# Local attention of a fused transformer kernel: values held stationary, probabilities divided before they are transposed, q's inverse norm applied inside the exponential

## The reference, cut to what matters

```python
q, k, v = split(shift_token(x) @ wqkv)            # 3 x 512 columns
q = l2norm(q) * qs;  k = l2norm(k) * ksc          # norm over the 64 of a head
q, k = rotary_xpos(q, k)                          # q*cos*scale + rotate_half(q)*sin*scale, k likewise
sim  = einsum(q * 8.0, look_around(k))            # 64 queries against 128 keys of two windows
sim  = where(mask, -max, sim)
attn = softmax(sim)
o    = einsum(attn, look_around(v))
x    = x + o @ wo
```

## Time and profile before

| | |
|---|---|
| time, three runs | 1675.93, 1677.23 (median), 1678.6 us |
| the profiled execution's own time | 1680.32 us |
| its span | 1678.5 us |
| PE busy | 1360.0 us (81%) |
| DVE busy | 1211.6 us (72%) |
| POOL busy | 887.5 us (53%) |
| ACT busy | 875.7 us (52%) |
| local attention | two stretches: first projections at 765.2 and 1216.7 us, about 370 us each |

### The profile page before, as it was taken

One profiled execution on the slowest core, in us unless ns is written; L12 is line 12 of the kernel. 1 busy time (PEld: TensorE's weight loads), 2 busy tenths in 40 slices (PEclk: granted clock), 3 DMA queues, 4 the chain that ended last, 5 costly groups with the idle time before them and its releaser, 6 DMA issues. The chain is left out here.

```text
span 1678.5 us, 26415 instructions
## 1 busy us (share of the span) xinstructions
PE 1360.0 (81%) x9350; PEld 645.6 (38%) x9412; DVE 1211.6 (72%) x1912; ACT 875.7 (52%) x1677; POOL 887.5 (53%) x980
## 2 busy tenths in 40 slices
PE   2368989989999775775899999968779999998597
PEld 1112222222222123452555555543335555555333
DVE  6268888888888643346888888858578888888484
ACT  1126666667666563224666666633145666665422
POOL 0866766667676101115877777710087777777000
PEclk9659999999999998887999999998989999999898
DMA  3333332333333101001111111101011111000001
GB/s 90 75 57 70 58 70 58 70 65 69 70 58 70 26 1 50 1 2 36 24 24 24 24 24 24 24 1 41 13 29 24 24 24 24 22 21 22 1 0 52
DMA packets 161398, 61.14 MB, mean 36 GB/s; under 512 B 139722, under 2 KB 153076, under 8 KB 161268
## 3 DMA queue, kind: packets, MB, share of 16 engines
q1 hardware_dynamic: 161268, 59.45, 16.8%
HBM read 8.73 MB, written 2.10 MB: 6 GB/s over the span
## 5 line engine op out<-in xcount | busy, mean ns | idle before, releaser
L642 DVE TENSOR_REDUCE row_max<-max_ps 128x2 f32<-128x1024 f32 x256 | 313.0, 1223 | 73.7 <-PE max_ps L514 72.3
L673 ACT ACTIVATE prob<-scores_ps 128x1024 f32<-128x1024 f32 x256 | 262.1, 1024 | 149.3 <-PE scores_ps L494 145.9
L1628 POOL TENSOR_TENSOR la_turned<-la_raw,lw_rot 128x1024 f32<-128x1024 f32 x64 | 154.9, 2420 | 183.4 <-ACT la_raw L1533 156.9
L1285 PE MATMUL la_ring<-lw_wqkv,la_hT 128*128 128x512 f32 x384 | 200.8, 636 | 46.2 <-DVE la_hT L1402 27.4
L494 PE MATMUL scores_ps<-stack 128*128 128x512 f16 x512 | 156.2, 387 | 41.8 <-ACT prob L673 40.9
L1523 ACT ACTIVATE la_prob<-la_s,la_neg_max 128x128 f32<-128x128 f32 x512 | 156.4, 391 | 52.7 <-DVE la_neg_max L1447 52.7
L1635 POOL TENSOR_TENSOR la_turned<-la_turned,la_swapped 128x1024 f32<-128x1024 f32 x64 | 151.1, 2361 | 21.4 <-DVE la_swapped L1429 16.8
L528 PE MATMUL heads_ps<-prob,v_pad 128*32 128x512 f32 x1024 | 138.1, 612 | 1.1 <-ACT prob L673 1.1
L514 PE MATMUL max_ps<-stack 24*128 24x512 f16 x512 | 102.7, 398 | 30.0 <-DVE row_max L642 17.6
L1639 POOL TENSOR_TENSOR la_turned<-la_turned,la_inv 128x1024 f32<-128x1024 f32 x64 | 121.8, 1904 | 5.0
L494 PEld LDWEIGHTS scores_ps<-stack 128*128 128x128 f16 x512 | 34.2, 97 | 209.3 <-ACT prob L673 160.7
(11 more groups left out here) (156 smaller groups left out, 2803.3 us busy)
## 6 DMA issues: line engine op xcount, KB each, us to landing
la_v_back<-la_v_own SPq DMA_DIRECT2D x112, 130.0 KB, 2.3
X<-in_x SPq DMA_DIRECT2D x8, 256.0 KB, 5.0
stack<-stack_tok SPq DMA_TRANSPOSE x128, 3.2
out<-X SPq DMA_DIRECT2D x8, 256.0 KB, 2.5
lw_wqkv<-in_wqkv SPq DMA_DIRECT2D x2, 768.0 KB, 4.6
stack<-shift_row SPq DMA_DIRECT2D x64, 2.0 KB
lw_rot<-in_rot SPq DMA_DIRECT2D x2, 512.0 KB, 6.4
lw_w<-in_fw SPq DMA_DIRECT2D x2, 341.0 KB
```

What stands on the lines that cost most here:

```text
L642: nc.vector.tensor_reduce(row_max[:, grp % 2, w // 2, :, w % 2], max_ps[:], AX.X, ALU.max).then_inc(max_made, 1)
L673: nc.scalar.activation(prob[:, c % 4, 2 * pr:2 * pr + 2, :], scores_ps[:], ACT.Exp, scale=1.0 / LOGIT_SCALE).then_inc(exp_made, 1)
L1285: nc.tensor.matmul(ring_ps[:, r % 2, :], hT[:, b % 2, t * P:(t + 1) * P], wqkv[:, use * INNER:(use + 1) * INNER], start=True, stop=True).t ...
L1628: nc.gpsimd.tensor_tensor(spun, raw[:, T % 2].rearrange("p s (h f) -> p s h f", f=LD), rot[:, T % TPB, :, 0, :].unsqueeze(2).to_broadcast( ...
```

## The change

It does six things, all in `local_attention`:

1. The weighing has v stationary (64 columns) and the transposed probabilities moving (64 columns); the result comes out transposed already, heads on partitions. The ones column, `take_out`, `o_tok` and the transpose of `o_tok` (L1459, L1464, L1393) are gone. ACT copies `o_ps` to `oT` once both halves are weighed.
2. The row sums come from the exponential's accumulator output (`accum_out`). A new step `share` on DVE inverts the 8 sums and multiplies the probabilities by them in two halves, ahead of the transposes.
3. q is no longer multiplied by its inverse norm on POOL; the exponential takes it as a scale, and a new small DVE instruction multiplies the maxima by it to get the bias. POOL's last multiply is for k alone (half the elements), and POOL's order is cosines, add, polish, multiply.
4. The clip of the sums of squares is a `scalar_tensor_tensor` with a second tensor of -0.5 in place of a `tensor_scalar`.
5. Every engine's order inside the slot is new. PE: scores, q transposes, probability transposes, k transposes, first half of weighing, q projection, (`wo`), second half of weighing, k and v projections, (mean). DVE: share, maxima and bias, qT, probT, norms, (batch end), rotate, (subtract), (hT). ACT: squares, (variance), two exps, kT, two exps, q raw, two exps, oT, k raw, two exps, v, Ln and Exp, (square).
6. The ring's order of uses, semaphores and counts follow; `inv` has four buffers, `oT` one.

The core of the diff:

```diff
@@ scores, transposes, weighing (PE)
+                if use == TURN_Q:
+                    pe.wait_ge(added_rot, T + 1)
+                else:
                     pe.wait_ge(scaled, T + 1)
...
-                pe.wait_ge(exp_made, T + 1)
                 for half in range(2):
+                    pe.wait_ge(shared, 2 * T + half + 1)
...
-                        mm = nc.tensor.matmul(o_ps[64 * w:64 * w + 64, j, 0:LD + 1],
-                                              probT[:, 4 * half + j, 64 * w:64 * w + 64],
-                                              (v_back, v_own)[w][:, at, 4 * half + j, :], start=True, stop=True)
+                            mm = nc.tensor.matmul(o_ps[64 * e:64 * e + 64, pair, 64 * w:64 * w + 64],
+                                                  (v_back, v_own)[w][:, at, h, :],
+                                                  probT[:, h, 64 * w:64 * w + 64], start=True, stop=True)
...
-                    for c in range(4):
-                        mm = nc.tensor.transpose(m_ps[:, c * P:(c + 1) * P],
-                                                 o_tok[:, c * P:(c + 1) * P], ident[:])
@@ DVE
-                nc.vector.tensor_scalar(sumsq[:, par], sumsq[:, par], 1e-24, -0.5, ALU.max,
-                                        ALU.mult).then_inc(clip_made, 1)
+                nc.vector.scalar_tensor_tensor(out=sumsq[:, par], in0=sumsq[:, par], scalar=1e-24,
+                                               in1=minus_half[:], op0=ALU.max, op1=ALU.mult
+                                               ).then_inc(clip_made, 1)
...
+                nc.vector.tensor_tensor(bias[:, T % 2].rearrange("p (c e) -> p c e", e=2),
+                                        neg_max[:, T % 2].rearrange("p (e c) -> p c e", e=2),
+                                        inv[:, T % 4, 0:LH].rearrange("p (c e) -> p c e", e=2),
+                                        ALU.mult).then_inc(bias_made, 1)
+
+            def share(T):
+                par = T % 2
+                dve.wait_ge(exp_made, T + 1)
+                nc.vector.reciprocal(inv_sum[:], sums[:, par]).then_inc(inv_sum_made, 1)
+                dve.wait_ge(inv_sum_made, T + 1)
+                for half in range(2):
+                    heads = slice(4 * half, 4 * half + 4)
+                    nc.vector.tensor_tensor(prob[:, par, heads], prob[:, par, heads],
+                                            inv_sum[:, heads].unsqueeze(2).to_broadcast([P, 4, KEYS]),
+                                            ALU.mult).then_inc(shared, 1)
@@ ACT
-                                               bias=neg_max[:, T % 2, place(h):place(h) + 1])
+                                               bias=bias[:, T % 2, h:h + 1], scale=inv[:, T % 4, h:h + 1],
+                                               accum_out=sums[:, T % 2, h:h + 1])
...
+                    act.wait_ge(o_filled, 2 * (O + 1))
+                    nc.scalar.activation(oT[:, :, t * P:(t + 1) * P], o_ps[:], ACT.Copy).then_inc(oT_made, 1)
@@ POOL
-                polish(T)
                 pool.wait_ge(plain_made, T + 1)
                 pool.wait_ge(swap_made, T + 1)
                 nc.gpsimd.tensor_tensor(turned[:, T % 2], turned[:, T % 2], swapped[:],
                                         ALU.add).then_inc(added_rot, 1)
+                polish(T)
...
-                heads = turned[:, T % 2].rearrange("p s (h f) -> p (s h) f", f=LD)
+                heads = turned[:, T % 2, 1].rearrange("p (h f) -> p h f", f=LD)
```

More of the change, by code:

```diff
@@ L1204, in run, with ring_tile, ring_count, m_count @@
             over(slot, T_LAST)
-        RING = 5 * 8
+        TURN_Q, TURN_K, PROJ_Q, PROJ_K, PROJ_V = range(5)
         def ring_index(T, use):
-            return 5 * T + use if use < 3 else 5 * (T + 2) + use
+            return 5 * (T + 2) + use if use < 2 else 5 * T + use
+        def ring_tile(r):
+            return r // 5 - 2 * (r % 5 < 2)
         def ring_used(r):
[L1212 to L1226, removed]
+            return 0 <= ring_tile(r) < NT
+        def ring_count(T, use):
+            r = ring_index(T, use)
+            return sum(ring_used(x) for x in range(r + 1))
+        W0, MEAN, SQUARE = 1, 2, 3
+        def m_count(b, step):
+            return 3 * b + step
         def ended(T):
@@ L1472, in slot @@
                     shift(dve, hT[:, 0, :], batch_at(XT, 0), h_made)
-                if N is not None:
-                    norms(N)
+                if O is not None:
+                    share(O)
                 if U is not None:
                     maxima(U)
-                if N is not None:
-                    rotate(N)
-                if O is not None:
-                    take_probT(O, 0)
-                    take_probT(O, 1)
-                b = ended(n - 5)
-                if b is not None:
-                    x = batch_at(XT, b)
-                    dve.wait_ge(m_filled, m_count(n - 5) + 1)
-                    nc.vector.tensor_tensor(x, m_ps[:], x, ALU.add).then_inc(x_added, 1)
-                if O is not None:
-                    take_out(O, 0)
-                if b is not None:
-                    dve.wait_ge(x_added, b + 1)
-                    shift(dve, shifted, x, sh_made)
                 if R is not None:
-                    r = ring_index(R, 3)
-                    dve.wait_ge(ring_filled, r + 1 - missing(r))
+                    r = ring_index(R, TURN_Q)
+                    dve.wait_ge(ring_filled, ring_count(R, TURN_Q))
                     if R - 1 > 0:
@@ L1499, in slot @@
                 if O is not None:
-                    take_out(O, 1)
+                    take_probT(O, 0)
+                    take_probT(O, 1)
+                if N is not None:
+                    norms(N)
+                b = ended(n - 5)
+                if b is not None:
+                    x = batch_at(XT, b)
+                    dve.wait_ge(m_filled, m_count(b, W0))
+                    nc.vector.tensor_tensor(x, m_ps[:], x, ALU.add).then_inc(x_added, 1)
+                    dve.wait_ge(x_added, b + 1)
+                    if b > 0:
+                        dve.wait_ge(c_made, b)
+                    shift(dve, shifted, x, sh_made)
+                if N is not None:
+                    rotate(N)
                 if b is not None:
                     dve.wait_ge(sh_made, 2 * (b + 1))
-                    dve.wait_ge(m_filled, m_count(n - 5) + 2)
+                    dve.wait_ge(m_filled, m_count(b, MEAN))
                     nc.vector.tensor_tensor(batch_at(C, b), shifted[:], m_ps[:],
@@ L1553, in slot @@
                 if U is not None:
-                    exps(U, range(3, 6))
+                    exps(U, range(4, 6))
+                if O is not None:
+                    b, t = O // TPB, O % TPB
+                    act.wait_ge(o_filled, 2 * (O + 1))
+                    if b > 0 and t == 0:
+                        act.wait_ge(m_filled, m_count(b - 1, W0))
+                    nc.scalar.activation(oT[:, :, t * P:(t + 1) * P], o_ps[:], ACT.Copy).then_inc(oT_made, 1)
                 if T is not None:
```

225 lines of the change are left out of this document (104 added, 121 removed).

## The result

The changed kernel takes 1739.56 us (median; 1729.94 to 1741.58) against 1676.58 for the kernel before: ratio 1.0365, 95% interval 1.033 to 1.04. The forecast was slower, 1726, range 1664 to 1790.

The account below looks back on a forecast made before the run. DVE and POOL holding each other up under the lock bound the kernel, not PE. 4 x 10.0 + 4.8 + 0.7 = 45.5 us a batch against 42.43, +3.1 times 16 = +49: 1729, less 3 gives 1726; range 1664 to 1790.

Parts of the forecast that it names:

- The lock: DVE instructions reading two SBUF tensors and POOL tensor_tensors exclude each other, longest-waiting first; need about 9.0 to 9.4 us a tile.
- the first rival: The lock spares the new DVE instructions: plain tile 9.05 to 9.3 us, total 1649 (or 1669); chance 0.17.
- The plain tile: The attention tile that took 9.21 us before, without batch-end work or hT shift; forecast 10.0, +0.8.
- Two level rings: Plain tile's repeating chains, POOL and DVE under the lock against exponentials, scores and maxima: level at 9.9 to 10.05 us.
- B+9.4: Plain tile's last exponential ends 9.4 us after B, the time at which POOL's add ends.
- Share's wait for the add: DVE's share is held from the last exponential until POOL's add ends, finishing 1.2 us after it.
- GpSimd's ring: Kernel before: POOL's chain (2.36, wait 0.70, polish, 2.36, 1.90 us) alone sets the plain tile's period of 9.21.
- The exponential: ACT's pitch between exponentials: 0.25 us before, 0.45 to 0.50 taken; scale +0.10, accumulator output nothing to 0.21.
- Rival 2: ACT's accumulator read dear, pitch 0.60 to 0.70 us; bias misses its turn; plain tile 11 to 11.3; 1797; chance 0.15.
- The wo tile: Batch's end: wo ahead of second weighing, residual add and shift ahead of DVE's rotation, which ends 4.8 us later.
- The hT tile: Tile with the hT shift behind DVE's rotation: second half held by POOL's add, only +0.7 us stays.
- rival 3: Bias misses its turn once a batch, in the hT tile: +37 us over the forecast, 1763; chance 0.17.

Follow-up runs that it names:

- experiment 6: Changed kernel with GpSimd's last multiply cut from 64 numbers a head to 1, so k is normalised in one column only: 1876.74 us, ratio 1.1194.
- experiment 7: Kernel before with only the new clip, scalar_tensor_tensor with a tensor of -0.5: 1680.7 us against 1676.15.
- Experiment 5: Changed kernel without share, the division of the probabilities by the row sums; accumulator kept: 1682.29 us, ratio to before 1.0023.
- experiment 1: Changed kernel without accum_out on the exponentials, the sums being constant ones: 1716.31 us, ratio to before 1.0229.
- experiment 2: Changed kernel with q's projection ahead of the first half of the weighing on TensorE: 1705.74 us, ratio to before 1.0166.
- Experiment 8: Kernel before with q's inverse norm as the exponential's scale and GpSimd's last multiply for k alone; no accumulator: 1683.95 us against 1675.87.
- Experiment 3: Changed kernel with VectorE's rotation ahead of the batch-end residual add and shift: 1713.62 us, ratio to before 1.0213.
- experiment 4: Changed kernel with both the rotation ahead of the batch-end block and q's projection ahead of the first weighing: 1689.13 us, ratio to before 1.0082.

## Why the prediction was right, step by step

- **The lock** (rows 4): shown. Bias and clip behave as the share's and the rotation's kind (experiments 6 and 7); the first rival, that it spares the new instructions, is out. In the prediction this was the step on which the sign hung. Experiment 5 bears it out as far as it goes: without share the loss is all but gone. How much of share's cost is the lock and how much its own 1.3 us was not separated.
- **The plain tile, +0.8 forecast, +1.0 measured.** Two level rings were forecast; both are there. From the add's end (951.68) the last exponential ends at 961.5, +9.8 against B+9.4 forecast, and experiments 1 and 2 lay bare the other ring at 9.88, where 9.9 stood in the working. The mis-sized terms: polish's first instruction started only at 952.32, as its seed from ACT came late, and share held it until B+1.27; so k's multiply started at B+2.31 instead of B+1.95, it is 1.04 long and not 0.95, and the bias was free at B+3.35, not B+2.95. From the last exponential to the next maxima it is 1.83, not 1.65.
- **Share's wait for the add**: wrong for the plain tile of the changed kernel (1.29, unheld: the exponentials ended so late that share came just as the add ended); right once the other ring was shortened (2.12 in experiment 2). That share ended at B+1.19, where B+1.2 was forecast, is luck of this kind: it came late and did not wait.
- **The kernel before.** The working took GpSimd's ring as the period, with no other near it. Experiment 8 relieved GpSimd by 0.86 a tile and got 9.44 for 9.21: TensorE's order was near, and the reading of the old period did not reckon with it.
- **The exponential**: pitch 0.44 to 0.45, the low edge of the 0.45 to 0.50 taken, 0.25 before. Experiment 1 splits the 0.19 into 0.09 for the scale operand (0.10 taken from the earlier trace rows) and 0.10 for the accumulator. The accumulator's cost in time is 23 us (experiment 1), 0.32 on a plain tile where 8 x 0.10 would be 0.8; that half of the exponentials lie where ACT waits for the projection anyway is the reason given for it, and was not tested by itself. Rival 2 did not come.
- **The wo tile, +4.8 forecast over a plain one, +4.85 measured.** That the number fits is in part luck. The working had the late rotation as the path that counts (+4.8), and the one over oT as clearly shorter. Experiment 3 took the rotation out and the tile fell by 1.0 only: the second path stands at +3.85. Moving q's projection gave 1.0 too, and leaving out share 2.0, which waits for the add there, as the working had it for every tile.
- **The hT tile, +0.7 forecast, +0.4 measured.** The bias did not miss its turn there: rival 3 was out, though experiment 6 shows how near its mechanism lay.
- **The clock**: I had it at 0.95 or more. The mean is 1.00 over layer 0's tiles and 0.97 over layer 1's, but it fell to its lower level for a few us in five batches of layer 1 (4 x 1.38 and 1.7), about 7 us that were not in the sum.
- **The sum.** From the first maxima to the last, layer 0 takes 26.7 us more than before and layer 1 34.0: 60.7, of which about 7 are the clock and about 53 the tiles, where 49 were forecast. It is +3.65 on a full batch instead of +3.1, but only six of a layer's eight are full: in layer 0 the first four distances add 0.35 and the last three 4.5, so that the layer counts as 7.3 batches and not as 8. The two errors partly cancel. The profiled executions differ by 57.8 us (1680.32 and 1738.16) and the medians by 63; the few us between these figures and the 60.7 lie outside the attention tiles or in the spread of the executions.

The pieces do not add up to the loss: leaving out share gives back 57 us, the two moves of experiment 4 50, the accumulator 23, of 63 in all. They work on the same two rings, so what one gives another cannot give again.

Where the expected savings of the change went: POOL's 0.86 a tile turned into a wait for DVE (2.19 idle before the add); the four transposes of PE into idle time (busy 78% of the stretch, 87% before); take_out's time on DVE was spent on share.

## What to carry to other kernels

Before moving work between VectorE and GpSimd, add up what both need under the lock, with every VectorE instruction that reads two tensors from SBUF, and look at the others too (the `tensor_scalar` of one tensor was held as well: the clip of the kernel before 1.52 us, the second half of the hT shift 2.46). Then look which long GpSimd instruction is in flight when a short one on the critical chain is issued: 8 numbers can cost 2 us. Taking work away from GpSimd can make a kernel slower, when its next long instruction thereby gets ahead of a short one that everything waits for. When several rings are within a few tenths of each other, as in this kernel, a saving need not show at its size, and a gain in one tile must be looked for in the next one before it is believed.

## What the runs showed of the hardware that was not expected

- The accumulator's output is an instruction of its own on ScalarE, 0.19 to 0.26 us for 128x1 (mean 210 ns over 512), which overlaps its neighbours so that it adds about 0.10 to the pitch:

```profile
L1525 ACT ACTIVATION_READ_ACCUMULATOR la_prob<-la_s,la_bias,la_inv 128x1 f32 x512 | 107.4, 210 | 0.0
```

- TensorE's granted clock fell from 1.00 to 0.50 within a stage in which it was busy 78% of the time, after idle stretches of 1.30 and 0.59 us, in layer 1 and not in layer 0 with the same instructions; in the kernel with GpSimd's multiply cut, in which it was busy 72% of the time, the mean over the stretch was 0.89.
- On GpSimd a 128x512 multiply with a broadcast operand takes 1.04 us where the 128x1024 one took 1.90: more than half.
